# Row destinations as integers in the row buffer, seven row buffers, and the last batch's row scatters two to a tile, in a fused attention and top-2 experts kernel

## The reference

```python
x = x + conv_attention(channel_layernorm(x))      # 8 heads, 1024 tokens a batch, gated output
t = to_tokens(x)                                  # 8192 tokens of 128 floats
t = t + experts(token_layernorm(t))               # below
x = from_tokens(t)

def experts(xt):
    logits = xt @ Wr + br
    top_p, top_idx = top_k(softmax(logits), 2)    # two of eight experts
    weights = top_p / top_p.sum(-1)
    xn = layernorm(xt)                            # the scale and shift of each expert follow
    h = gelu(einsum('end,edh->enh', xe, W1) + b1) # 128 -> 512
    y = einsum('enh,ehd->end', h, W2) + b2        # 512 -> 128
    return (weights * y[top_idx]).sum(1)
```

## Time and profile before

| | us |
|---|---|
| median of 3 runs | 2870.46 |
| lowest and highest of the 3 | 2868.31, 2876.31 |
| the profiled execution | 2866.05 |
| its span (first to last instruction) | 2864.3 |
| PE busy in the span | 2762.0 |
| DVE / ACT / POOL busy | 2279.5 / 1465.8 / 1388.0 |
| POOL `send` (L710), 156 issues | 183.4 |
| POOL `index` (L703), 39 operations | 16.3 |

### The profile page before, as it was taken

One profiled execution on the slowest core, in us unless ns is written; L12 is line 12 of the kernel. 1 busy time (PEld: TensorE's weight loads), 2 busy tenths in 40 slices (PEclk: granted clock), 3 DMA queues, 4 the chain that ended last, 5 costly groups with the idle time before them and its releaser, 6 DMA issues.

```text
span 2864.3 us, 50916 instructions
## 1 busy us (share of the span) xinstructions
PE 2762.0 (96%) x20202; PEld 2592.1 (90%) x20202; DVE 2279.5 (80%) x3471; ACT 1465.8 (51%) x1883; POOL 1388.0 (48%) x1049
## 2 busy tenths in 40 slices
PE   6999999999999999999999999999999999998996
PEld 5899989998999999998999899989999899987786
DVE  6777798778978888878877897889877888866563
ACT  3455445553555345544555355544554455566671
POOL 4344533545445533643355534653364335547783
PEclk9999999999999999999999999999999999999998
DMA  2555030102102121202111210202110211146786
GB/s 110 208 189 222 18 101 23 33 25 96 38 26 72 45 63 43 65 17 100 45 30 56 88 46 25 73 30 78 23 47 10 96 34 31 57 139 216 226 266 213
DMA packets 99794, 238.04 MB, mean 83 GB/s; under 512 B 20088, under 2 KB 24770, under 8 KB 99558
## 3 DMA queue, kind: packets, MB, share of 16 engines
q1 hardware_dynamic: 90470, 217.85, 23.3%
q0 software_dynamic: 9088, 16.94, 1.7%
HBM read 131.23 MB, written 105.30 MB: 83 GB/s over the span
## 4 chain that ended last, share of the span: by engine, by line
PE 72%; DVE 10%; POOL 7%; issue 5%; ACT 4%; DMA 1%; another core or an unknown queue 1%; SPq 0%; POOLq 0%; DVEq 0%; ACTq 0%
PE PV L752 48%; PE MX L752 12%; PE ST L752 11%; POOL yrows L710 3%; DVE E L1566 1%; DVE rt L1571 1%; ACT xr L1217 1%; DVE ul L1525 1%; ACT h L1217 1%; DVE E L1567 1%; POOL acc L639 1%; DVE mcol L1601 1%; DMA y<-yrows 1%; DVE vt L1549 1%
## 5 line engine op out<-in xcount | busy, mean ns | idle before, releaser
L639 POOL TENSOR_TENSOR acc<-acc,tmp 128x256 f32<-128x256 f32 x512 | 803.8, 1570 | 1199.6 <-DVE tmp L1616 1197.6
L1217 ACT ACTIVATE Eh<-ST 128x1024 fp32r<-128x1024 f32 x512 | 525.4, 1026 | 734.8 <-PE ST L752 734.8
L1601 DVE TENSOR_REDUCE mcol<-MX 128x1 fp32r<-128x1024 f32 x512 | 625.5, 1222 | 238.9 <-PE MX L752 238.2
L752 PE MATMUL PV<-vh,Eh 128*128 128x258 f32 x4096 | 766.2, 289 | 0.0
L752 PE MATMUL PV<-vh,El 128*128 128x258 f32 x4096 | 746.1, 284 | 0.0
L752 PE MATMUL PV<-vl,Eh 128*128 128x256 f32 x4096 | 736.2, 281 | 4.4 <-DVE vl L1596 4.4
L752 PEld LDWEIGHTS PV<-vh,Eh 128*128 128x128 f32 x4096 | 631.1, 190 | 50.6 <-issue 6.7
L1606 DVE TENSOR_TENSOR El<-E,Eh 128x1024 fp32r<-128x1024 f32 x512 | 643.4, 1257 | 0.4
L752 PEld LDWEIGHTS PV<-vl,Eh 128*128 128x128 f32 x4096 | 597.7, 189 | 6.1 <-DVE vl L1596 6.1
L752 PEld LDWEIGHTS PV<-vh,El 128*128 128x128 f32 x4096 | 596.8, 190 | 0.0
L1217 ACT ACTIVATE E<-ST 128x1024 f32<-128x1024 f32 x512 | 521.3, 1018 | 0.0
(11 more groups left out here) (264 smaller groups left out, 3340.7 us busy)
## 6 DMA issues: line engine op xcount, KB each, us to landing
rows<-xr SPq DMA_DIRECT2D x68, 520.0 KB, 6.2
stk<-rt SPq DMA_DIRECT2D x64, 512.0 KB, 2.8
kst<-stk SPq DMA_DIRECT2D x192, 128.0 KB
qst<-stk SPq DMA_DIRECT2D x192, 128.0 KB
wt<-wall SPq DMA_DIRECT2D x39, 514.0 KB
wt<-wall SPq DMA_DIRECT2D x39, 512.5 KB
xrow<-rows SPq DMA_DIRECT2D x39, 260.0 KB
y<-yrows SPq DMA_DIRECT2D x32, 256.0 KB, 4.6
```

The lines of the kernel that those rows point to most:

```text
L639: nc.gpsimd.tensor_tensor(acc[:, ic, :], acc[:, ic, :], tmp[:, p, :], ALU.add).then_inc(s_acc, 1)
L752: return nc.tensor.matmul(o, w, m, start=start, stop=stop)
L1217: return nc.scalar.activation(o, i, func, **kw)
L1601: nc.vector.tensor_reduce(mcol[:, k % 2, p:p + 1], MX[:, :], AX, ALU.max).then_inc(s_red, 1)
```

## The change

1. **The destination is an integer in the row.** The code in column C of a row is now the destination itself, stored as int32 in the float buffer (batch rows by `iota` and `tensor_copy`; padding rows get 2*NTOK by an `iota` over `xr[0]`). `send` takes its offsets straight from `xrow`. `index`, the `idx` buffers and the semaphore t_ix are gone; `send` waits for t_x and t_yw.
2. **Seven row buffers** (XR 6 to 7) at the same look-ahead of four tiles (AHEAD = 4, formerly XR - 2). Since the offsets lie in `xrow`, load_x(j) now waits until the scatter of tile j-7 has landed (t_sc), where it waited for `yrow` and `idx` of tile j-6.
3. **SP's order in a step** is load_w(0, j+2), load_w(1, j+1), load_x(j+4).
4. **SPREAD**: the 16 row scatters of the last batch go two after each of send(9) to send(16), where they went three after each of send(8) to send(12) and one after send(13).

```diff
-XR = 6
+XR = 7
+AHEAD = 4
-SPREAD = [8, 8, 8, 9, 9, 9, 10, 10, 10, 11, 11, 11, 12, 12, 12, 13]
+SPREAD = [9, 9, 10, 10, 11, 11, 12, 12, 13, 13, 14, 14, 15, 15, 16, 16]
...
             def load_x(j):
-                wait(sp, t_yw, j - XR + 1)
-                wait(sp, t_ix, j - XR + 1)
+                if j >= XR:
+                    wait(sp, t_sc[(j - XR) % YR], 64 * ((j - XR) // YR + 1))
...
             for j in range(NT):
-                if j == NFULL - XR + 2:
+                if j == NFULL - AHEAD:
                     wait(sp, t_list, 4)
                 if j + 2 < NT:
                     wait(sp, t_gl, 4 * j + 4)
                     load_w(0, j + 2)
-                ahead = j + XR - 2
+                if j + 1 < NT:
+                    wait(sp, t_ye, j)
+                    load_w(1, j + 1)
+                ahead = j + AHEAD
                 if ahead < NFULL or NFULL + 1 < ahead < NT:
                     load_x(ahead)
                 if ahead == NFULL + 1:
                     for i in range(2):
                         wait(sp, s_sc[i], 16 * KC * B)
                     for i in range(2):
                         load_x(NFULL + i)
-                if j + 1 < NT:
-                    wait(sp, t_ye, j)
-                    load_w(1, j + 1)
...
+            nc.gpsimd.iota(xr[0][:, :, C].bitcast(i32), [[0, KC]], base=2 * NTOK, channel_multiplier=0).then_inc(s_const, 1)
-            nc.gpsimd.iota(code[:, :, :], [[-NTOK, 2], [-P, KC]], base=2 * NTOK, channel_multiplier=-1,
+            nc.gpsimd.iota(code[:, :, :], [[NTOK, 2], [P, KC]], base=0, channel_multiplier=1,
...
-            def index(j):
-                wait(pool, t_x[j % XR], 16 * (j // XR + 1))
-                if j >= XR:
-                    wait(pool, t_sc[(j - XR) % YR], 64 * ((j - XR) // YR + 1))
-                nc.gpsimd.tensor_scalar(idx[j % XR][:, :], xrow[j % XR][:, :, C], -1.0, float(2 * NTOK),
-                                        ALU.mult, ALU.add).then_inc(t_ix, 1)
-
             def send(j):
+                wait(pool, t_x[j % XR], 16 * (j // XR + 1))
                 wait(pool, t_yw, j + 1)
-                wait(pool, t_ix, j + 1)
                 for i in range(4):
                     nc.gpsimd.indirect_dma_start(
-                        out=yrows_d[:, :], out_offset=bass.IndirectOffsetOnAxis(ap=idx[j % XR][:, i:i + 1], axis=0),
+                        out=yrows_d[:, :], out_offset=bass.IndirectOffsetOnAxis(ap=xrow[j % XR][:, i, C:C + 1].bitcast(ui32), axis=0),
...
-            index(0)
-            index(1)
             for j in range(NT):
-                if j + 2 < NT:
-                    index(j + 2)
```

More of the change, by code:

```diff
@@ L225, in build @@
         xrow = [keep(f"xrow{i}", [P, 4, ROW], f32) for i in range(XR)]
-        idx = [keep(f"idx{i}", [P, 4], ui32) for i in range(XR)]
         xnh = [keep(f"xnh{i}", [P, NB], f32r) for i in range(2)]
@@ L359, in build @@
         t_yw = sem("t_yw")
-        t_ix = sem("t_ix")
         t_sc = [sem(f"t_sc{i}") for i in range(YR)]
@@ L438, in fill @@
                 if i == 0:
-                    wait(sp, s_const, 10)
+                    wait(sp, s_const, 11)
                 sp.dma_start(rows_d[i * FILL:(i + 1) * FILL, :].rearrange("(p r) c -> p (r c)", r=KC),
@@ L525, in _ @@
                 wait(sp, s_sc[i], 16 * KC * (B - 1))
-            for j in range(XR - 2):
+            for j in range(AHEAD):
                 load_x(j)
             for j in range(NT):
-                if j == NFULL - XR + 2:
+                if j == NFULL - AHEAD:
                     wait(sp, t_list, 4)
@@ L697, in _, with send @@
                 batch(b)
-            def index(j):
+            def send(j):
                 wait(pool, t_x[j % XR], 16 * (j // XR + 1))
-                if j >= XR:
-                    wait(pool, t_sc[(j - XR) % YR], 64 * ((j - XR) // YR + 1))
-                nc.gpsimd.tensor_scalar(idx[j % XR][:, :], xrow[j % XR][:, :, C], -1.0, float(2 * NTOK),
-                                        ALU.mult, ALU.add).then_inc(t_ix, 1)
-            def send(j):
                 wait(pool, t_yw, j + 1)
-                wait(pool, t_ix, j + 1)
                 for i in range(4):
                     nc.gpsimd.indirect_dma_start(
-                        out=yrows_d[:, :], out_offset=bass.IndirectOffsetOnAxis(ap=idx[j % XR][:, i:i + 1], axis=0),
+                        out=yrows_d[:, :], out_offset=bass.IndirectOffsetOnAxis(ap=xrow[j % XR][:, i, C:C + 1].bitcast(ui32), axis=0),
                         in_=yrow[j % YR][:, i, :], in_offset=None, bounds_check=2 * NTOK - 1, oob_is_err=False
                         ).then_inc(t_sc[j % YR], 16)
-            index(0)
-            index(1)
             for j in range(NT):
-                if j + 2 < NT:
-                    index(j + 2)
                 if j == PAIRED:
@@ L1730, in route @@
                     tt(xr[1][:, :, C + 1], r_e[:, :], xr[0][:, :, C + 1], ALU.mult).then_inc(s_rk, 1)
-                    nc.vector.tensor_copy(xr[0][:, :, C], code[:, 0, :]).then_inc(s_rk, 1)
-                    nc.vector.tensor_copy(xr[1][:, :, C], code[:, 1, :]).then_inc(s_rk, 1)
+                    nc.vector.tensor_copy(xr[0][:, :, C].bitcast(i32), code[:, 0, :]).then_inc(s_rk, 1)
+                    nc.vector.tensor_copy(xr[1][:, :, C].bitcast(i32), code[:, 1, :]).then_inc(s_rk, 1)
                 if s == 41:
                     wait(dve, s_rk, base + 48)
-                    ts(code[:, :, :], code[:, :, :], float(-TOK), None, ALU.add).then_inc(s_rk, 1)
+                    ts(code[:, :, :], code[:, :, :], float(TOK), None, ALU.add).then_inc(s_rk, 1)
                     tt(r_c[all3], r_o1[all3], r_sl[all3], ALU.mult).then_inc(s_rk, 1)
```

## The result

| | us |
|---|---|
| before, median of 5 runs on the same chip | 2870.46 |
| after, median of 5 runs (lowest and highest) | 2888.53 (2886.57, 2893.9) |
| ratio after to before, 95% interval | 1.0060 (1.0046 to 1.0073) |
| profiled execution after, its span | 2893.9, 2892.2 |
| the same kernel measured again later, median of 10 runs (lowest and highest) | 2878.38 (2870.48, 2887.82) |

The change makes the kernel slower, by 0.6% in the first measurement and by 0.4% in the second. The forecast was 2874.0 us with a range up to 2886; the first measurement lies above it. The second lies inside, but the kernel before came out at 2867.27 us beside it, so it is 11.1 us more where the forecast had 3.6 more. The intervals meet between 1.0046 and 1.0052; why single executions of one program spread over 17 us is part of what follows.

What follows compares the result with a forecast made beforehand. PE was taken to bound the FFN stage's second half, something else its first stretch. Terms -1.5, +3.1 and +2.0 sum to +3.6 us, giving 2874.0 us on the median, with an 8-in-10 range of 2866 to 2886.

Steps and rivals of the forecast that it cites:

- The row scatters: Spread over send(9) to send(16), the last lands later, so tile 21 waits and is transposed later: +3.1 us.
- What bounds the kernel: In the FFN stage, PE bounds the second half at 6.44 us a tile; something else bounds the first stretch.
- The integer destination: Removing POOL's 39 `idx` operations is hidden under PE until the end, where the last send starts earlier: -1.5 us.
- rival A: PE's late signals return under POOL's unbroken issuing and hold up the sends too: +10, 2880.5 us, chance 0.27.
- Seven buffers and the wait on landing: In the steady stretch, row loads waiting for landed scatters end their wait about when they did before: nothing.
- The landing: A row scatter's write to DRAM takes 2.08 us, perhaps more; each microsecond goes straight into tile 21's delay.
- Rival B: DVE's low-part operations lengthen two POOL issues a tile, 13.9 us instead of 7.2: +10.3, 2880.8 us, chance 0.10.
- The lost 20.1 us: Time lost between tiles 9 and 16; whether late signals stay away or return, waiting for rows replaces it: nothing.
- The clock: PE restarts at the lower clock after standing still before tile 21, with nothing hiding it: +2 us (1.4 to 3.5).

Runs made afterwards that it cites:

- e8: The changed kernel itself, unaltered, measured again: 2878.38 us, ratio 1.0037 to the kernel before.
- e9: The changed kernel with a one-element POOL operation ahead of each send and between each send and its row scatters: 2876.67 us, ratio 1.0033.
- e10: e9 with the old table of row scatters: 2870.76 us, ratio 1.0014.
- e5: The kernel before with a small POOL operation after every second indirect DMA in tiles 8 to 13: 2870.94 us, ratio 1.0011.
- e6: The kernel before with a small POOL operation between the send and the row scatters of tiles 8 to 13: 2868.52 us, ratio 1.0003.
- e2: The changed kernel with the old table of row scatters: 2878.92 us, ratio 1.0032.
- e3: The kernel before with only the new table of row scatters: 2875.82 us, ratio 1.0023.
- e1: The changed kernel with a POOL operation of the old idx's size (128x4, result unused) ahead of each send: 2878.21 us, ratio 1.0031.
- e7: The changed kernel with a one-element POOL operation ahead of each send: 2877.13 us, ratio 1.0032.
- e12: e10 with nine row buffers instead of seven, result buffers unchanged at five: 2881.3 us, ratio 1.0029.
- e11: e10 with nine row buffers and seven result buffers: 2876.17 us, ratio 1.0026.
- e13: e11 with a one-element POOL operation after every single indirect DMA: 2892.07 us, ratio 1.0068.

## Why the prediction was wrong

Two terms of the sum failed. The row scatters, put at +3.1 us, made tile 21 11.2 us later in the profiled execution after and 11.7 in e8's (2694.36 against 2682.63). The removal of `idx`, put at -1.5, went with late signals behind tile 21 in the first of these executions and not in the second. Of the second measurement's 11 us the table accounts for some 6 (e9 against e10); the 4 by which e10 still lies above the kernel before have no cause that was shown.

**What bounds the kernel: read too short.** "The second half of the stage is thus bound by PE" holds for PE's windows, but POOL, 118 of these 142 us busy, was as full: with a gap of 0.30 us at each issue it had a single pause, 3.33 us, between send(8) and the end. So in the kernel before, and in e5 and e6, POOL's own work sets the end. Without `idx` POOL has some slack: e2 pauses for 15.8 us and still takes 214.4 us from send(8) to its last issue, where before took 216.6. What reaches the end there is the delay of tile 21, since PE is gapless behind it (e3, e8, e9), and POOL pauses for 8 to 9 us around it in every run with the new table (9.31, 8.88), since POOL and PE wait for each other. The table alone (e3) costs 7 us.

**The integer destination, -1.5 us: wrong in size and sign in the first measurement.** "Each is hidden under PE and worth nothing" held for the time of `idx`, not always for its place: an operation between the sends also ended a train of issues, and without it late signals came behind tile 21 in some executions. In the profiled execution after, 16.7 us are lost behind tile 21, where the late signals are; e1 and e7, which put an operation back, lose 2.3 and 2.5 us between tile 21 and the end of the span (e1: 2878.6 - 2694.6 = 184.0 against 181.7). In e8's execution, the same program without late waits there, this part is 2874.8 - 2694.4 = 180.4 us, 18.0 less than in the first and 1.3 shorter than before, where the text had -1.5 for the end and +2 for the clock: there the term was not too hopeful.

**The row scatters, +3.1 us: the mechanism right, the size 11.2.** Tile 21 waits for the last row scatter as forecast. Against the steps of the text the profiled execution has: send(9) at 2613.76 instead of 2611.5, +2.3, all of it there before the FFN stage; a pause of 6.85 in place of 0.30, +6.6, which is rival A's mechanism, priced there and not taken; lengthened issues of 6.6 instead of 7.2 us, -0.6; landing and SP 3.96 instead of 2.83, +1.1; load to transposes 2.83 instead of 4.0, -1.2. Together +8.2. In e9, without late signals, the way from send(9) to tile 21 is 2689.80 - 2613.74 = 76.1 us where the text had 74.2: the working of the chain was sound, its start and the pause were not.

**Seven buffers and the wait on landing, nothing: not settled.** In e10 SP's row loads wait 10.2 us for landed scatters between 2604 and 2700 us, where the kernel before has no such wait, and PE waits for the weights behind them; e12 took most of PE's wait away and gained nothing.

**The landing.** "Each microsecond goes straight into the sum" was right: 1.1 us in the profiled execution and 0.2 in e9 (2686.93 - 2683.89 = 3.04 instead of 2.83).

**Rival B fell.** By the lock that the Trainium skill describes (SBUF — State Buffer, section "SBUF: two separate sides"), two issues a tile would last longer, 13.9 us in all. In the profiled execution the 47 steps from send(9) to the last row scatter take 73.27 us; less 47 x 1.28 = 60.16 and the pause's 6.55 that is 6.6 us. The lock itself agrees with the trace: single issues last 1.87 us instead of 0.97 beside DVE's low-part operations. While late signals hold DVE up too, there is less to hold POOL up: in e9, without them, the same steps take 70.15 us, 10.0 more than 60.16 with its small operations counted in, still short of 13.9.

**The lost 20.1 us: nothing.** The total was right: e6 takes the late signals out and gains nothing, e9 gains some 2 us beside e8's median. The reason given holds in the changed kernel, where e9's PE waits 16.86 us for the rows of tile 21 instead; in the kernel before it is POOL's work (e6). In the profiled execution, though, they took part through POOL's pause.

**The clock, +2 us.** Right: the twelve matmuls behind the wait, and the transposes, in the chain of after:

```profile
2693.82 1.11 PE MX L1003 x4
2694.93 4.92 PE ST L743 x12
```

4.92 us against 2.8 in the tiles behind, 2.1 more, and 0.5 more in the transposes (1.11 against 0.60).

## What to carry to other kernels

Look for the bound by an engine's pauses, not by its busy share: an engine that issues DMAs with fixed gaps can be full at 83% busy, and then taking waits away from another engine brings nothing (e6). Whether a new pause of it is paid depends on whether its work was made less at the same time (e2). Before moving work behind a hand-over (here, row scatters that a later tile must see), count what the issuing queue does between the first and the last of them. An operation that looks hidden can still matter by standing between others; take it out alone first, in several executions, when single runs of a kernel spread.

## What the runs showed of the hardware that was not expected

PE's semaphore signals can arrive late while POOL issues indirect DMAs in long trains (ACT's longest wait for one is 11.4 us, in e11); from 2604 to 2830 us no semaphore rise of ACT or DVE is recorded over 0.5 us late in any of the executions, and the last of the waits end 1.5 to 1.7 us after POOL falls idle (three times in after). In e9 a one-element POOL operation between groups of at most four, some 0.05 us each, took 52.2 us of such waits (after; 23.5 in e8) to none. Four were not enough where POOL worked off a backlog (e11, 31.1 us); one was (e13, 0.6 us). Trains of eight to twelve without any such wait occur too (e8 behind tile 21). Whether the length of the train or the density of the issues decides is not settled. A one-element POOL operation that meets DVE's two-input operation takes 0.5 us or more instead of 0.18 (up to 1.22 in e13), where an issue takes 1.87 instead of 0.97.
